# First layer's masked attention scores as four 64-row matmuls over two PSUM banks, with masked queries of four heads in place of eight

## What is computed

```python
b = jnp.cumsum(gc, axis=-2)
qe = qc * jnp.exp(b)
A = jnp.einsum('bhik,bhjk->bhij', qe, kc * jnp.exp(-b)) * mask
o = jnp.einsum('bhck,bhkv->bhcv', qe, S) + jnp.einsum('bhij,bhjv->bhiv', A, vc)
S = jnp.exp(bl[:, :, 0, :])[..., None] * S + jnp.einsum('bhck,bhcv->bhkv', kc * jnp.exp(bl - b), vc)
```

## Time and profile before

| | us |
|---|---|
| median of 3 runs | 2944.18 (2941.35 to 2947.05) |
| the profiled execution | 2944.93 |
| its span in the trace | 2943.1 |
| PE busy | 2656.3 (90%) |
| DVE busy | 2352.8 (80%) |
| ACT busy | 2074.1 (70%) |
| POOL busy | 1987.8 (68%) |

### The profile page before, as it was taken

How to read it: one execution, slowest core, us unless ns; L and a number is a source line. 1 busy time by engine, 2 the same in 40 slices (tenths; PEclk the granted TensorE clock), 3 DMA queues, 4 the chain that set the end, 5 groups by cost and what they waited for, 6 DMA issues and landing times.

```text
span 2943.1 us, 58655 instructions
## 1 busy us (share of the span) xinstructions
PE 2656.3 (90%) x17318; PEld 2095.7 (71%) x17318; DVE 2352.8 (80%) x5975; ACT 2074.1 (70%) x4670; POOL 1987.8 (68%) x1699
## 2 busy tenths in 40 slices
PE   6899999987499684797999999999999999999997
PEld 3566666755399563676787887887878878788786
DVE  4567766774677487686999999998999999999896
ACT  3455444442466465464999999998999999999996
POOL 3222223235344125654899999998999999999998
PEclk8799999998799897898999999999999999999999
DMA  5456665569466455567877866667667567566663
GB/s 149 128 180 209 200 200 180 192 198 297 126 200 187 157 185 174 161 192 223 252 235 231 249 211 208 215 206 232 199 203 231 197 205 230 196 225 205 195 216 115
DMA packets 322100, 588.35 MB, mean 200 GB/s; under 512 B 48784, under 2 KB 141232, under 8 KB 321296
## 3 DMA queue, kind: packets, MB, share of 16 engines
q1 hardware_dynamic: 307440, 545.07, 59.9%
q0 software_dynamic: 14352, 39.54, 3.7%
HBM read 464.45 MB, written 124.17 MB: 200 GB/s over the span
## 4 chain that ended last, share of the span: by engine, by line
POOL 32%; issue 9%; PE 7%; ACT 3%; DVE 2%; DMA 1%; POOLq 1%; SPq 0%; DVEq 0%; ACTq 0%
POOL mm L2799 7%; POOL y L2812 7%; POOL y_lo L2805 6%; POOL yz L2816 6%; POOL y L2826 6%; PE bank L65 1%; PE bank L67 1%; PE bank L66 1%; ACT mt L2729 1%; PE bank L2630 1%; DVE cv L2882 1%; PE bank L2622 1%; PE bank L2639 1%; DMA wi<-ssm_wi_split 1%; POOLq L2475 1%
## 5 line engine op out<-in xcount | busy, mean ns | idle before, releaser
L2799 POOL TENSOR_TENSOR mm<-mt,cb 128x512 f32<-128x512 f32 x384 | 492.3, 1305 | 57.6 <-ACT mt L2749 54.8
L2729 ACT ACTIVATE mt<-a_wide,a_tok 128x128 f32<-128x128 f32 x1536 | 487.2, 389 | 3.4 <-POOL mm L2799 2.6
L2882 DVE SCALAR_TENSOR_TENSOR cv<-bank,taps,cv 128x509 f32<-128x509 f32 (+2 forms) x576 | 429.6, 746 | 13.6
L65 PE MATMUL bank<-f,wi 128*128 128x512 f32 x768 | 321.4, 419 | 15.8 <-DMA wi<-ssm_wi_split 15.8
L67 PE MATMUL bank<-f,wi 128*128 128x512 f32 x768 | 305.3, 398 | 0.0
L66 PE MATMUL bank<-f,wi 128*128 128x512 f32 x768 | 305.0, 397 | 0.0
L2816 POOL TENSOR_TENSOR yz<-y,zs 128x512 f32<-128x512 f32 x192 | 249.0, 1297 | 15.1
L1020 POOL TENSOR_TENSOR early_rounded<-l_s_raw,early_rounded 128x768 fp32r<-128x768 f32 x33 | 60.8, 1842 | 283.6 <-ACT early_rounded L865 283.6
L2805 POOL TENSOR_TENSOR y_lo<-yz,y_hi 128x512 fp32r<-128x512 f32 x192 | 246.8, 1285 | 7.8 <-ACT y_hi L2754 6.1
L2812 POOL TENSOR_TENSOR y<-t 128x512 f32<-128x512 f32 x192 | 246.4, 1284 | 0.0
L2622 PE MATMUL bank<-mm,x_tok 128*64 128x128 f32 x3072 | 226.8, 283 | 13.4 <-POOL mm L2799 13.3
(11 more groups left out here) (481 smaller groups left out, 7889.3 us busy)
## 6 DMA issues: line engine op xcount, KB each, us to landing
wi<-ssm_wi_split SPq DMA_DIRECT2D x192, 512.0 KB, 4.9
a_wide<-a_scratch SPq DMA_DIRECT2D x192, 512.0 KB
l_fw<-ffn_split SPq DMA_DIRECT2D x72, 768.0 KB, 6.4
ea<-ea_scratch SPq DMA_DIRECT2D x384, 128.0 KB, 3.2
wo<-ssm_wo_split SPq DMA_DIRECT2D x192, 256.0 KB, 3.8
sorted_scratch<-early_plain SPq DMA_DIRECT2D x96, 130.5 KB
ssm_wi_split<-early_rounded SPq DMA_DIRECT2D x24, 512.0 KB
x_all<-sorted_scratch SPq DMA_DIRECT2D x94, 130.5 KB
```

Of the source, the lines that this page charges most:

```text
L65: pe.matmul(out, wh, xh, start=first, stop=False)
L2729: i = act.activation(mt[:, h, chunk(j)], a_wide[:, g % R, h, chunk(j)], ACT.Relu, bias=a_tok[:, s * NJ + j, 2 * t + h:2 * t + h + 1], scal ...
L2799: pl.tensor_tensor(mm[:, :, ts], mt[:, :, ts], cb[:, js, :].rearrange("p j t -> p (j t)") .unsqueeze(1).broadcast_to([P, 2, TS // 2]), ALU ...
L2882: dve.scalar_tensor_tensor(cv[:, a:TS], bank[:, X, 0:TS - a], taps[:, t, k:k + 1], cv[:, a:TS], ALU.mult, ALU.add).then_inc(ph["tap"], 1)
```

## The change

The masked queries hold four heads. Features 0 to 63 belong to heads 0 to 3 and features 64 to 127 to heads 4 to 7. A new mask `own_head` (128 x 4, the sum of the two halves of `headmask`, made once on DVE) keeps for each feature its own head within its half, and POOL's product is 128 x 256. `scores` multiplies each half of the features by itself: per chunk two matmuls of 64 rows x 64 columns with 256 moving columns, r = 0 into bank 2 and r = 1 into bank 3, at four different positions of the array for the two chunks. `masked_scores` reads the first 256 columns of both banks, 512 elements per partition as before. Since bank 3 is written, `scores` of j = 0 waits for `klt`, ACT's copy out of that bank.

```diff
@@ layer0
+        HR = H0 // 2
+        own_head = sb("own_head", [P, HR])
...
-        qb = part([P, 4, H0, CH])
-        raw = qb[:].rearrange("p a h c -> p (a h c)")
+        qb_whole = part([P, 4, H0, CH])
+        qb = qb_whole[:, :, 0:HR, :]
+        raw = qb_whole[:].rearrange("p a h c -> p (a h c)")
...
+                dve.tensor_tensor(own_head[:], col("headmask")[:, 0:HR], col("headmask")[:, HR:H0], ALU.add)
...
                 def scores(c, j):
                     if j == 0:
                         done(pe, "ke", c)
+                        done(pe, "klt", c)
                     else:
                         done(pe, "um", c * NC0 + 2 * j - 1)
                     done(pe, "qb", c * NC0 + 2 * j + 1)
                     for u in range(2):
                         n = 2 * j + u
-                        i = pe.matmul(bank[ROWS[u], 2, :], ke[:, n * CH:(n + 1) * CH],
-                                      qb[:, n % 4].rearrange("p h c -> p (h c)"), start=True, stop=True)
+                        for r in range(2):
+                            i = pe.matmul(bank[ROWS[u], 2 + r, 0:HR * CH], ke[ROWS[r], n * CH:(n + 1) * CH],
+                                          qb[ROWS[r], n % 4].rearrange("p h c -> p (h c)"), start=True, stop=True,
+                                          tile_position=(r * CH, u * CH))
                     i.then_inc(ph["a_ps"], 1)
...
-                    pl.tensor_tensor(qb[:, n % 4], qe[:, n * CH:(n + 1) * CH].unsqueeze(1).broadcast_to([P, H0, CH]),
-                                     col("headmask").unsqueeze(2).broadcast_to([P, H0, CH]), ALU.mult).then_inc(ph["qb"], 1)
+                    pl.tensor_tensor(qb[:, n % 4], qe[:, n * CH:(n + 1) * CH].unsqueeze(1).broadcast_to([P, HR, CH]),
+                                     own_head[:].unsqueeze(2).broadcast_to([P, HR, CH]), ALU.mult).then_inc(ph["qb"], 1)
...
-                    dve.tensor_tensor(am[:], bank[:, 2, :].rearrange("p (h c) -> p h c", h=H0),
-                                      col("causal64").unsqueeze(1).broadcast_to([P, H0, CH]), ALU.mult).then_inc(ph["am"], 1)
+                    dve.tensor_tensor(am[:].rearrange("p (r h) c -> p r h c", r=2),
+                                      bank[:, 2:4, 0:HR * CH].rearrange("p r (h c) -> p r h c", h=HR),
+                                      col("causal64").unsqueeze(1).unsqueeze(1).broadcast_to([P, 2, HR, CH]), ALU.mult).then_inc(ph["am"], 1)
```

## The result

The changed kernel takes 2953.12 us (median of 18 executions, 2946.27 to 2961.91), the kernel before, executed beside it, 2946.51 (18, 2940.23 to 2954.45). The ratio is 1.0023, 95% interval 1.0014 to 1.0032: slower by 6.7 us, give or take 2.7. The forecast was slower by 8.8. The profiled execution of the changed kernel, 2961.91 us with a span of 2960.1, is the highest of its 18, so single durations are read from it and totals from the medians.

What follows compares the result with a forecast made beforehand. PE was taken to bound beats 2 to 6. Terms 5.3 - 2.2 - 0.4 + 0.1 = +2.8 us, plus +6.0 for the clock, took 2944.93 to 2953.7, or 2953.0 in medians; range 2945 to 2959.

Steps and rivals of the forecast that it cites:

- rival (a): Clock behind the j = 0 gap holds, or falls in one or two beats: 2947.0, up to 2950; chance 0.31.
- The pair: Scores' matmuls on PE, from start to next matmul: 0.60 us in place of 1.01, 0.41 less per pair.
- The wait at j = 0: Beats 2 to 6: PE idle 2.7 us until ACT's klt copy ends, updates 1.88 us later.
- j = 1 and 2: Beats 2 to 6: nothing is waited for at updates, so PE gains 0.41 us each.
- j = 3: Beats 2 to 6: shorter scores only lengthen PE's wait for am, 0.8 in place of 0.4; gain nought.
- Beats 2 to 6 without the clock: Each beat 1.06 us longer from the wait less the gains; five beats +5.3.
- The clock: Half clock for some 3.4 us behind the j = 0 gap in 3.5 of five beats, +6.0 us.
- Beat 0: Latency chain without feed-forward work, half clock for j = 1 to 3: shorter pairs gain 2.2 us.
- Beat 1: PE's 4.45 us wait for DVE takes in loss and gains: nought, bounds -0.8 and +1.9.
- Beat 7: PE's 5.07 us wait for am covers the later scores, slack covers a fall; only j = 1 gains, -0.4.
- (b): The klt copy ends before turn does, so the wait costs nothing: 2937.6, faster; chance 0.04.
- (c): The four tiles don't run side by side, a pair takes 1.20 us: 2967.4; chance 0.08.

Runs made afterwards that it cites:

- e3: Changed kernel with scores of j = 0 put behind gate_up, so without the wait for klt; 2946.23 against 2952.21 for the kernel before, 0.9977.
- e4: Changed kernel with ten unused matmuls filling the gap ahead of the wait for klt; 2953.35 against 2952.21 for the kernel before, 1.0007.
- e6: e3 with POOL's product eight heads wide again, half of it unused; 0.9985 against the kernel before.
- e5: The kernel before again, no edit, for a second profile; ratio 1.0001.
- e2: The kernel before with only the added wait of scores at j = 0 for klt; 2971.32 us, 1.0056 against the kernel before.
- e1: The changed kernel again, no edit; 2959.06 against 2952.21 for the kernel before, 1.0023.
- e9: The changed kernel a third time, no edit, for another profile; 1.0014 against the kernel before.
- e7: e3 with down(f, 0) moved ahead of updates at j = 0; 2937.03 against 2950.23 for the kernel before, 0.9955.
- e11: e7 with down also ahead of updates at j = 3; 0.9973 against the kernel before.
- e8: The kernel before with only the reordering of e3, scores of j = 0 behind gate_up; 1.0004 against the kernel before.
- e10: e7 with sixteen unused matmuls ahead of the wait for am at j = 0 in beat 7; 0.9949 against the kernel before.

## Why the prediction was right, and where it was not

The total was right: slower by 6.7 us (ratio 1.0023) where 8.8 was said, and the mechanism, a wait plus a fall of the clock behind it, is shown by e3 and e4. The working behind it was right in part only, and that the total came out well is partly luck. The forecast had falls in three beats or more; measured were two, one and two, which is what rival (a) allowed ("or comes in one or two beats", up to 2950). The time went above (a)'s by falls in other places and by beat 7, which neither had in its sum. By its own steps, with the averages of the three changed profiles against the two of before:

**The pair: right.** 0.59 us, said 0.60; that the four tiles might not overlap (1.20) is refuted, and full overlap (0.50) was too low. The row of `updates` with two tiles was the good guide.

**The wait at j = 0: right.** Idle 2.66 us, said 2.7; `updates` 1.83 later, said 1.88; the copy of `klt` ends 380.06 - 376.90 = 3.16 us after `turn` starts, before 373.27 - 370.08 = 3.19: it doesn't move, as said.

**j = 1 and 2: right.** From `updates` of j = 0 to that of j = 2, two steps of (399.68 - 383.70) / 2 = 7.99 us; before, one started 8.44 after the other (383.49 - 375.05). That is 0.45 each, said 0.41.

**j = 3: wrong.** The prediction said that a shorter `scores` only makes the wait for `am` longer, 0.8 in place of 0.4, gain nought, because `am`'s chain begins with the work of t = 3. The wait is 0.41 as before, and the step from j = 2 to j = 3 is 408.16 - 399.68 = 8.48. In the kernel before it was 8.89: 0.41 gained. The step that failed stands in another sentence: "POOL's masked queries become half as wide; ... nobody in the steady beats waits for them". Nobody waits for them, but DVE's work ends later when POOL works beside it. DVE's subtraction `l_h_lo` stands ahead of `am` in DVE's queue. The rows of DVE and POOL in beat 4, first of the kernel before:

```profile
393.44 2.23 POOL L996 TENSOR_TENSOR early_plain<-early_plain,tab 128x512 f32<-128x512 f32 x2
395.63 2.36 POOL L1052 TENSOR_TENSOR l_base<-l_x_odd,l_xn 128x1024 f32<-128x1024 f32 x1
...
396.33 2.74 DVE L1337 TENSOR_TENSOR l_h_lo<-l_xn,l_h_hi 128x1024 fp32r<-128x1024 f32 x1 [1.64 <-ACT l_h_hi L880]
```

then of the changed kernel, and of it also the row that gathers all eight subtractions (ns, shortest/median/longest):

```profile
401.63 1.38 POOL L1003 TENSOR_TENSOR early_plain<-early_plain,l_own_head 128x256 f32<-128x256 f32 x2
402.97 2.37 POOL L1059 TENSOR_TENSOR l_base<-l_x_odd,l_xn 128x1024 f32<-128x1024 f32 x1
...
404.53 1.88 DVE L1345 TENSOR_TENSOR l_h_lo<-l_xn,l_h_hi 128x1024 fp32r<-128x1024 f32 x1 [1.64 <-ACT l_h_hi L887]
```

```profile
L1345 DVE TENSOR_TENSOR l_h_lo<-l_xn,l_h_hi x8: 1225/1882/1916, 153.8 to 729.5; 128x1024 fp32r<-128x1024 f32 x8
```

and of e6, the changed form with a wide product:

```profile
390.16 2.25 POOL L1006 TENSOR_TENSOR early_plain<-early_plain,l_own_head 128x512 f32<-128x512 f32 x2
392.37 2.39 POOL L1062 TENSOR_TENSOR l_base<-l_x_odd,l_xn 128x1024 f32<-128x1024 f32 x1
...
393.08 2.77 DVE L1348 TENSOR_TENSOR l_h_lo<-l_xn,l_h_hi 128x1024 fp32r<-128x1024 f32 x1 [1.64 <-ACT l_h_hi L890]
```

The reader is to see ends, not starts. POOL's addition `l_base` ends at 397.99, 405.34 and 394.76; DVE's subtraction ends at 399.07, 406.41 and 395.85, each time 1.07 to 1.09 later. The subtraction takes 1.225 us at the least (the gathering row), so it is as if it only got going when POOL was done. POOL's product is 2.23 us for two chunks with eight heads and 1.38 with four; so the addition starts, and ends, 0.85 earlier, and the subtraction shrinks from 2.74 to 1.88. In e6 it is back at 2.77, and PE's wait is 1.31: e6 settles that the step was POOL's. Counted from the start of `scores` of j = 2 (387.96, 396.15 and 384.68), POOL's product starts 5.48 us later in all three, and `updates` of j = 3 follows after 12.86, 12.01 and 12.90. So with the wide product the 0.45 of j = 2 would have been lost again at j = 3, where the step in e6 is 9.37 against 8.89 before; the narrow product is worth some 0.85 a beat. The Trainium skill (SBUF — State Buffer, SBUF: two separate sides) has the rule: DVE and GpSimd share a pair of ports as an exclusive lock, which an operation of DVE with two inputs in SBUF and one of GpSimd that reads SBUF hold for the whole instruction. The rows agree with its exclusion to 0.15 us (1.07 to 1.09 where the subtraction takes 1.225 at the least), and it was not drawn on for the prediction.

**Beats 2 to 6 without the clock: over-sized for that reason.** By rows: 1.83 - 0.45 - 0.45 - 0.41 = +0.52; by beats without falls: (79.23 + 79.13 + 78.87) / 3 = 79.08 against 78.40, the mean of beats 2 to 4 before and in e5: +0.7. Said: +1.06. Five beats +3.4 in place of +5.3.

**The clock: the cause right, the count too high.** Said: 3.5 falls in five beats of 3.4 us each, +6.0. Measured behind the gap: 2, 1 and 2 falls, of which two lasted 6.8 us. Low time behind the gap is 10.2, 6.8 and 6.8 us, and half of the mean is 4.0 us per execution. The basis, "two of three gaps", was three rows, and was raised on the ground that the new gap is longer; 5 of 15 here and 5 of 5 in e2, behind the same gap, show that its length doesn't set the count by itself. The rest of the term came from falls in other places, of 3.4 us each, that the kernel before hasn't: near 263 and 523 (changed), 422 and 521 (e1) and 500 (e9), five in three profiles, half of which is 2.8 us for one. All five stand behind a shorter wait of PE, three for the weights `l_fw` (0.58, 1.14 and 0.71 us) and two for ACT's copy at the turn from beat 5 to 6 (1.36 and 1.27). Those of the changed profile:

```profile
262.11 0.50 PE L65 MATMUL bank<-l_h_hi,l_fw 128*128 128x512 f32 x1 [0.58 <-DMA l_fw<-ffn_split]
...
520.95 1.12 PE L671 MATMUL bank<-early_plain,tab 16*128 16x512 f32 x2 [1.36 <-ACT early_plain L909]
```

At the wait for ACT's copy the clock also falls in e2, e3, e4, e7 and e11 (waits of 1.01 to 1.35), and in e8, which has the old scores and no wait for `klt` (1.34); it holds in the kernel before, e5 and e6 (0.89, 0.80 and 1.06), and two waits for the weights, of 0.66 us in e4 and 0.81 in e6, passed without a fall, as did a wait for ACT of 1.16 one beat later in e10 and e11. So these falls belong neither to the new gap nor to the four tiles alone. Why ACT and the weights come later in some profiles isn't shown. The measured sum of beats 2 to 6 is 406.3 - 396.7 = +9.5, said +11.3.

The rule of the Trainium skill (TensorE: Matmul & The Clock Gate, HAM oscillation), by which the clock holds behind such a gap (the rival (a)), was contradicted by 5 of 15 gaps in the changed kernel and 5 of 5 in e2. That rival had 0.31; what speaks for that much is that two of three gaps do pass without a fall.

**Beat 0: right.** -2.7 us, said -2.2. e6, with the wide product, gives 1.9 of it back (68.99 against 67.1, the mean of e3, e4 and e7), so POOL seems to have a hand in it here too, and not only the shorter pair as said; but one and the same kernel differs by 1.2 to 1.6 us here, so this isn't shown. **Beat 1: right**, 95.8 on average in both.

**Beat 7: wrong, and of the other sign.** Said: the slack covers the later `scores` and the fall, gain 0.4. From `turn` to the scatter it is 33.4 us in place of 29.85, +3.6. The wait itself is covered as said:

```profile
621.69 0.66 PE L609 MATMUL bank<-early_plain 64*64 64x256 f32 x8 [1.21 <-issue]
...
629.48 1.22 PE L622 MATMUL bank<-early_plain,l_klt 64*128 64x256 f32 x4 [4.14 <-DVE l_am L1089]
...
637.14 1.13 PE L609 MATMUL bank<-early_plain 64*64 64x256 f32 x8
```

but the fall behind it isn't like that of before. First the kernel before, then the changed one:

```profile
620.00:624.00 4.00, 4.00 (x21) 2.72 (x21) 2.61 (x6) 1.25 (x3) 3.79 (x3) 0.62 0.21 79
624.00:642.00 18.00, 16.01 (x125) 10.57 (x122) 15.74 (x32) 1.83 (x3) 5.03 (x6) 1.00 0.40 133
```

```profile
628.00:642.00 14.00, 12.52 (x67) 8.64 (x68) 8.61 (x17) 2.56 (x4) 4.39 (x5) 0.52 0.34 123
642.00:660.00 18.00, 15.57 (x138) 10.81 (x138) 14.04 (x29) 2.81 (x4) 4.49 (x5) 1.00 0.46 155
```

The clock comes back after 3.4 us before, and after 13.7 in the changed kernel: `updates`, `outputs` and the next `scores`, at 637.14, all run at half. What failed is the step "this covers the later `scores`": the wait covers them, but PE has the path from its end on. `updates` of j = 0 starts 9.5 to 9.6 us after `turn` in every profile, held by DVE; `updates` of j = 1, which waits for nothing, starts 9.84 later before and 13.50 in the changed kernel; and from there to POOL's copy ahead of the scatter (639.57 and 652.78) it is 9.81 and 9.80, and 9.8 in every other profile too (first the kernel before, then the changed one):

```profile
629.76 0.70 PE L615 MATMUL bank<-early_plain,l_klt 64*128 64x256 f32 x4
```

```profile
642.98 0.70 PE L622 MATMUL bank<-early_plain,l_klt 64*128 64x256 f32 x4
```

So the 3.6 us are PE's own work between the two `updates`, done at half clock for longer. In e7 that step is 10.44, since `down` was done in the wait and only what was left ran at half.

The long fall is in every kernel with four tiles and the old place of `down` (the changed one, e1, e9, e3, e4, e6: 13.7 us); it is 10.2 us in e7 and e11 and 6.8 in e10, and 3.4 in every kernel with two tiles (before, e5, e8 and e2). So it goes with the form of the scores and not with the wait for `klt`, as e3 shows, which hasn't this wait and has the long fall (33.6). Why the clock takes longer to come back is not settled.

**The sum.** Beat 0 -2.7, beat 1 nought, beats 2 to 6 +9.5, beat 7 +3.6, together +10.4; the layer ends 9.8 later in these profiles, and 6.7 us is the difference of the medians. The forecast of +8.8 lies between. The rivals: (b) fell with the copy's end at 380.06, (c) with the pair at 0.59. (a) is half right: its count of falls came, and with the clock held by filling (e4) the kernel is 1 to 2 us above the one before, where (a) said 2.8.

## What to carry to other kernels

A wait put on the head of an in-order queue is worth more than its length where the engine's clock falls behind an idle stretch. Reorder so that some independent work stands in it (e7: the wait gone and the next one filled, 13 us gained where the change alone cost 6.7), and price the fall as a chance out of many gaps, not of three; shorter waits, too, had falls behind them here (0.58 us at the least). When an operation gets shorter on an engine for which nobody waits, look at which other engine's operations overlap with it and end right behind it: their ends, compared over two kernels, show who holds up whom.

## What the runs showed of the hardware that had not been expected

- DVE's subtraction of two SBUF operands, 1.225 us at the least, takes 1.88 to 2.77 us beside POOL's operations and ends 1.07 to 1.09 us after POOL's addition whatever its own start (three kernels).
- Four 64 x 64 tiles with 256 columns of float32 take 0.59 us, where two of 128 x 64 with 512 took 1.01.
- The same gap of 2.62 to 2.67 us in the same kernel comes with a fall of the clock in some beats and not in others (5 of 15; 5 of 5 in e2), and the fall can begin while PE still stands (383.15 in e2). Waits of 0.58 to 1.36 us for weights or for ACT had falls behind them too, and others of 0.66 to 1.16 had none. The falls of beats 2 to 6 last 3.4 us or 6.8; that behind PE's wait in beat 7 lasts 3.4 with two tiles and 13.7 with four (10.2 or 6.8 in e7, e11 and e10).
- The same code behind the first layer took between 2185.4 and 2195.3 us over the profiles, so that a difference of 7 us can't be read off two single executions.
